# Half a part's weights turned as bf16 halves, and the accumulator scaled by VectorE

## The reference, cut to what matters

```python
h = maximum(layernorm(x), 0)
q, k, v = h @ Wq.T + bq, h @ Wk.T + bk, h @ Wv.T + bv
scores = where(adj > 0, q @ k.T / sqrt(128), -9e15)
x = x + elu(softmax(scores) @ v)            # first layer
h = maximum(layernorm(x), 0)
hw = h @ W                                   # second layer
e = where(adj > 0, leaky_relu(hw @ a1 + (hw @ a2).T), -9e15)
x = x + hw + softmax(e) @ h
```

## Time and profile before

| what | value |
|---|---|
| median of 3 timed runs | 785.39 us (780.93, 785.39, 785.89) |
| the profiled execution | 782.49 us, its span 780.7 us |
| TensorE, matmuls | 728.9 us busy, 93% of the span |
| TensorE, weight loads | 609.6 us, 78% |
| VectorE | 563.2 us, 72% |
| ScalarE | 559.9 us, 72% |
| GpSimd | 417.6 us, 53% |
| DMA | 130.86 MB, 168 GB/s over the span |

### The profile page before, as it was taken

One profiled execution on the slowest core, in us unless ns is written; L12 is line 12 of the kernel. 1 busy time (PEld: TensorE's weight loads), 2 busy tenths in 40 slices (PEclk: granted clock), 3 DMA queues, 4 the chain that ended last, 5 costly groups with the idle time before them and its releaser, 6 DMA issues. The chain is left out here.

```text
span 780.7 us, 18250 instructions
## 1 busy us (share of the span) xinstructions
PE 728.9 (93%) x6229; PEld 609.6 (78%) x6229; DVE 563.2 (72%) x1199; ACT 559.9 (72%) x1095; POOL 417.6 (53%) x317
## 2 busy tenths in 40 slices
PE   4976999999999999999999998585999999999996
PEld 2555888888888888888888887463888888888885
DVE  4857687878787878878787876498585585586572
ACT  5936678687878777777868787584967977977910
POOL 1058599999999999999999973243000000000000
PEclk9988999999999999999999999797999999999999
DMA  6059989999888898989898954650234334423100
GB/s 229 1 162 280 283 212 248 274 232 280 233 280 238 271 253 254 262 247 256 255 259 245 274 112 73 123 103 1 54 69 93 81 73 91 91 64 87 37 10 13
DMA packets 189323, 130.86 MB, mean 168 GB/s; under 512 B 170336, under 2 KB 176992, under 8 KB 181088
## 3 DMA queue, kind: packets, MB, share of 16 engines
q1 hardware_dynamic: 188544, 130.05, 61.4%
q10 hardware_dynamic: 576, 0.26, 0.1%
q0 software_dynamic: 160, 0.00, 0.0%
HBM read 69.47 MB, written 18.87 MB: 113 GB/s over the span
## 5 line engine op out<-in xcount | busy, mean ns | idle before, releaser
L1337 PE MATMUL ps_x<-v,big 128*128 128x258 bf16 x2048 | 232.0, 275 | 2.3 <-issue 2.3
L1337 PEld LDWEIGHTS ps_x<-v,big 128*128 128x128 fp8e4 x2048 | 198.9, 98 | 32.5 <-issue 2.4
L682 DVE CUSTOM_DVE_ANT_0 scores<-ps_s,mask_neg 128x1024 f32<-128x1024 f32 x128 | 155.7, 1217 | 25.5 <-POOL mask_neg L553 17.0
L538 POOL TENSOR_SCALAR mask_bytes<-adj_sb 128x2048 uint8<-128x2048 int32 x64 | 147.5, 2321 | 44.8 <-POOLq L79 40.9
L601 ACT ACTIVATE scores<-scores,neg_max 128x1024 f32<-128x1024 f32 x128 | 146.1, 1143 | 23.3 <-DVE neg_max L688 23.3
L701 DVE TENSOR_TENSOR low<-scores 128x1024 bf16<-128x1024 f32 x96 | 136.0, 1417 | 29.2 <-ACT scores L601 27.0
L553 POOL TENSOR_SCALAR mask_neg<-mask_bytes 128x2048 bf16<-128x2048 uint8 x64 | 150.6, 2354 | 5.4 <-POOL mask_bytes L538 0.4
L812 PE MATMUL ps_acc<-v_parts,hiT 128*128 128x256 bf16 x768 | 141.6, 274 | 5.4 <-DMA lowT<-low 5.1
L615 ACT ACTIVATE hiT<-ps_t 128x512 bf16<-128x512 bf16 (+1 forms) x128 | 103.0, 805 | 56.6 <-PE ps_t L793 54.0
L878 ACT ACTIVATE big<-s_block,s_col 128x512 fp8e4<-128x512 f32 x224 | 139.3, 714 | 0.0
L813 PE MATMUL ps_acc<-v_parts,lowT 128*128 128x128 bf16 x768 | 134.7, 220 | 0.0
(11 more groups left out here) (139 smaller groups left out, 997.3 us busy)
## 6 DMA issues: line engine op xcount, KB each, us to landing
adj_sb<-in_adj SPq DMA_DIRECT2D x64, 1024.0 KB, 5.3
mask_bytes_dram<-mask_bytes SPq DMA_DIRECT2D x32, 512.0 KB, 2.8
x_sb<-in_x SPq DMA_DIRECT2D x8, 256.0 KB, 7.7
out<-res SPq DMA_DIRECT2D x32, 64.0 KB, 1.5
lowT<-low SPq DMA_TRANSPOSE x96, 4.7
big<-mask_bytes_dram SPq DMA_TRANSPOSE x32, 4.5
raw_w<-in_L_gnn_Wq ACTq DMA_DIRECT2D x1, 64.0 KB, 3.1
raw_w<-in_L_gnn_Wk ACTq DMA_DIRECT2D x1, 64.0 KB, 3.6
```

What stands on the lines that cost most here:

```text
L538: nc.gpsimd.tensor_scalar(mask_bytes[b % 2][:, half(h)], adj_sb[h][:], 1.0, 0.0, ALU.min, ALU.max).then_inc(bytes_ready, 1)
L682: nc.vector.tensor_tensor_reduce(out=scores[bn % 2][:, part(k)], in0=ps_s[k % 2][:], in1=mask[bn % 2][:, part(k)], scale=1.0, scalar=LOWES ...
L1337: last = nc.tensor.matmul(ps_x[b % 2][k][:], by_key_tile(m, t)[:, b], v1[k][:, t, :].bitcast(BF16), start=(t == 0), stop=(t == T - 1))
```

## The change

The fourth part's second half (columns 3584 to 4095) is handled like the other parts. TensorE turns its bf16 high half with four bf16 transposes instead of four fp32 ones; VectorE makes its low half with a `low_part` of 512 columns (`low3`) before it is turned, and SP turns that by DMA (`lowT3`, 128 KB), issued ahead of the next strip's `lowT0`. Of the two `turned_low` of a strip one is left. `times_v(s, 1)` now waits for `lowT3`. `low_part(s+1, 0)` moves behind `add_mask(s+2, 1)`; `low_part(s+1, 3)` takes its place.

The accumulator is no longer copied by ScalarE. VectorE's `attended(s-1)` takes each half of it from PSUM with a scalar_tensor_tensor, which scales it by one over the sum and adds bv to the first and the first result to the second. It stands where `turned_low(s, 1)` stood. The next strip's first `times_v` waits for it (`att_ready`). GpSimd's `add_halves` is gone.

ELU's minus one is taken from x in the first stage, by GpSimd, a chunk of 512 columns at a time, once a chunk is normalised; `add_elu` no longer subtracts ones.

```diff
@@ -96,6 +96,10 @@
...
+            for c in range(NC if x_in else 0):
+                pool.wait_ge(h_ready, c + 1)
+                xs = x_sb[:, 4 * c:4 * c + 4, :]
+                nc.gpsimd.tensor_scalar(xs, xs, -1.0, None, ALU.add)
@@ -430,17 +434,18 @@
...
+            UNITS = ((3, slice(0, 512)), (3, slice(512, PART)), (0, slice(0, PART)), (1, slice(0, PART)),
+                     (2, slice(0, 512)), (2, slice(512, PART)))
...
+                hiT = [sb(c2, f"hiT{k}", [D, PART], BF16) for k in range(3)] + [sb(c2, "hiT3", [D, 512], BF16)]
+                low = [sb(c2, f"low{k}", [D, PART], BF16) for k in range(3)] + [sb(c2, "low3", [D, 512], BF16)]
+                lowT = [sb(c2, f"lowT{k}", [D, 8, D], BF16) for k in range(3)] + [sb(c2, "lowT3", [D, 4, D], BF16)]
@@ -493,11 +498,11 @@
                     def turn_low(c, b, k):
...
-                        sp.wait_ge(low_done, 3 * s + k + 1)
+                        sp.wait_ge(low_done, 4 * s + 1 + (1, 2, 3, 0)[k])
...
-                            sp.wait_ge(pv_done, 8 * s + 2 * k - 4)
+                            sp.wait_ge(pv_done, 8 * s + (-4, -2, 0, -6)[k])
@@ -506,6 +511,7 @@
...
+                    turn_low(0, 0, 3)
                     turn_low(0, 0, 0)
...
                         if has(c, b, 1):
+                            turn_low(*at(c, b, 1), 3)
                             turn_low(*at(c, b, 1), 0)
@@ -552,21 +559,10 @@
...
-                    def add_halves(s):
...
-                        nc.gpsimd.tensor_tensor(acc_sb[:, 0, :], acc_sb[:, 0, :], acc_sb[:, 1, :], ALU.add).then_inc(halves_added, 1)
...
-                        nc.gpsimd.tensor_tensor(att[:], acc_sb[:, 0, :], bv_rep[:], ALU.add).then_inc(att_ready, 1)
...
-                        steps = Steps(pool, pool_own, 2 * s)
+                        steps = Steps(pool, pool_own, s)
                         pool.wait_ge(att_exp_ready, s + 1)
-                        steps.do(nc.gpsimd.tensor_tensor(att_exp[:], att_exp[:], ones[:], ALU.subtract))
                         steps.do(nc.gpsimd.tensor_tensor(att_exp[:], att_exp[:], att_pos[:], ALU.add))
                         xs = x_sb[:, s, :] if isinstance(s, int) else x_sb[:, bass.ds(s, 1), :].rearrange("p o f -> p (o f)")
...
                 @block.scalar
...
-                    def copy_pT(s, i):
...
-                        nc.scalar.activation(pT_high[i][:], ps_t[i % 3][:], ACT.Copy).then_inc(pT_ready, 1)
...
-                    def acc_copy(s, b):
...
-                        nc.scalar.activation(acc_sb[:], ps_a[:], ACT.Copy, scale=inv_by_parity[:, b % 2:b % 2 + 1]).then_inc(acc_out, 1)
+                        k, half_of = UNITS[u]
+                        act.wait_ge(t_done, TURNS * s + 1 + u)
+                        wait(act, pv_done, 8 * s + (-7, -6, -4, -2, 0, 0)[u])
+                        if u == 0:
+                            nc.scalar.activation(pT_high[:], ps_t[0][:], ACT.Copy).then_inc(hiT_ready, 1)
+                        else:
+                            out = hiT[3][:] if u == 1 else hiT[k][:, half_of]
+                            nc.scalar.activation(out, ps_t[u % 3][:].bitcast(BF16)[:, half_of], ACT.Copy).then_inc(hiT_ready, 1)
@@ -688,24 +668,33 @@
...
                     def low_part(s, b, k):
                         dve.wait_ge(exp_done, 4 * s + EXP_ORDER.index(k) + 1)
                         wait(dve, lowT_in[k], 16 * s)
-                        p = scores[b % 2][:, part(k)]
+                        p = scores[b % 2][:, part(k) if k < 3 else slice(N - 512, N)]
                         nc.vector.tensor_tensor(low[k][:], p, high_half(p), ALU.subtract).then_inc(low_done, 1)
+                    def turned_low(s):
+
+                        dve.wait_ge(hiT_ready, TURNS * s + 1)
+                        nc.vector.tensor_tensor(pT_low[:], ps_t[0][:], pT_high[:], ALU.subtract).then_inc(pT_low_ready, 1)
+
                     def inverse_sum(s, b):
-                        steps = Steps(dve, own, s)
-                        steps.do(nc.vector.tensor_reduce(out=inv_sum[:, b % 2:b % 2 + 1], in_=row_sum[:, b, :], axis=AX.X, op=ALU.add))
-                        wait(dve, acc_out, s - 1)
-                        nc.vector.reciprocal(inv_by_parity[:, b % 2:b % 2 + 1], inv_sum[:, b % 2:b % 2 + 1]).then_inc(inv_ready, 1)
+                        steps = Steps(dve, own, 2 * s)
+                        steps.do(nc.vector.tensor_reduce(out=inv_sum[:, 0:1], in_=row_sum[:, b, :], axis=AX.X, op=ALU.add))
+                        steps.do(nc.vector.reciprocal(inv_by_parity[:, 0:1], inv_sum[:, 0:1]))
+
+                    def attended(s):
+
+                        dve.wait_ge(pv_done, 8 * s + 8)
+                        nc.vector.scalar_tensor_tensor(out=acc_sb[:], in0=ps_a[:, 1, :], scalar=inv_by_parity[:, 0:1],
+                                                       in1=bv_rep[:], op0=ALU.mult, op1=ALU.add).then_inc(acc_half, 1)
+                        wait(dve, att_exp_ready, s)
+                        dve.wait_ge(acc_half, s + 1)
+                        nc.vector.scalar_tensor_tensor(out=att[:], in0=ps_a[:, 0, :], scalar=inv_by_parity[:, 0:1],
+                                                       in1=acc_sb[:], op0=ALU.mult, op1=ALU.add).then_inc(att_ready, 1)
@@ -728,11 +718,12 @@
                         ahead, ahead2 = has(c, b, 1), has(c, b, 2)
                         if has(c, b, -1):
                             inverse_sum(s - 1, (b + 3) % 4)
-                        turned_low(s, 0)
+                        turned_low(s)
                         low_part(s, b, 1)
                         if ahead:
                             add_mask(s + 1, bn, 2)
-                        turned_low(s, 1)
+                        if has(c, b, -1):
+                            attended(s - 1)
                         low_part(s, b, 2)
                         if ahead:
                             add_mask(s + 1, bn, 3)
@@ -743,12 +734,15 @@
                             dve.wait_ge(epi_done, s - 2)
                             moments_of(s - 3)
                         if ahead:
-                            low_part(s + 1, bn, 0)
+                            low_part(s + 1, bn, 3)
                         if ahead2:
                             add_mask(s + 2, (b + 2) % 4, 1)
+                        if ahead:
+                            low_part(s + 1, bn, 0)
                     all_periods(dve, period)
                     inverse_sum(T - 1, 3)
+                    attended(T - 1)
@@ -768,47 +762,41 @@
...
-                    def turn(s, b, i):
...
-                            col = 512 * (6 + i) + D * t
-                            last = nc.tensor.transpose(ps_t[i % 3][:, D * t:D * t + D], scores[b % 2][:, col:col + D], ident[:])
...
                     def turn_high(s, b, u):
...
-                        k, tiles = ((0, range(8)), (1, range(8)), (2, range(4)), (2, range(4, 8)))[u]
+                        k, half_of = UNITS[u]
                         pe.wait_ge(exp_done, 4 * s + EXP_ORDER.index(k) + 1)
+                        wait(pe, hiT_ready, TURNS * s + u - 2)
                         if u == 0:
-                            wait(pe, hiT_ready, 4 * s)
-                        elif u < 3:
-                            pe.wait_ge(pT_low_ready, 2 * s + u)
-                        else:
-                            pe.wait_ge(hiT_ready, 4 * s + 1)
-                        out = ps_t[(2 + u) % 3][:].bitcast(BF16)
+                            for t in range(4):
+                                col = 512 * 6 + D * t
+                                last = nc.tensor.transpose(ps_t[0][:, D * t:D * t + D], scores[b % 2][:, col:col + D], ident[:])
+                            last.then_inc(t_done, 1)
+                            return
+                        if u == 3:
+                            pe.wait_ge(pT_low_ready, s + 1)
+                        out = ps_t[u % 3][:].bitcast(BF16)
                         high = high_half(scores[b % 2][:, part(k)])
-                        for t in tiles:
-                            last = nc.tensor.transpose(out[:, D * t:D * t + D], high[:, D * t:D * t + D], ident_half[:])
+                        for col in range(half_of.start, half_of.stop, D):
+                            last = nc.tensor.transpose(out[:, col:col + D], high[:, col:col + D], ident_half[:])
                         last.then_inc(t_done, 1)
                     def times_v(s, i):
                         j = PV_ORDER[i]
-                        if i < 2:
-                            pe.wait_ge(pT_low_ready, 2 * s + i + 1)
-                        else:
-                            pe.wait_ge(hiT_ready, 4 * s + (1, 1, 2, 2, 3, 4)[i - 2])
-                            if i % 2 == 0:
-                                pe.wait_ge(lowT_in[j // 2], 16 * s + 16)
+                        pe.wait_ge(hiT_ready, TURNS * s + (1, 2, 3, 3, 4, 4, 5, 6)[i])
                         if i == 0:
```

(43 more changed lines are left out.)

33 lines of the change are left out of this document (5 added, 28 removed).

## The result

The changed kernel takes 811.98 us (median of four runs, 806.04 to 815.85), the one before beside it 784.08: a ratio of 1.035, 95% interval 1.028 to 1.043. It is slower, by more than the forecast's whole range. Its profiled execution took 806.04 us, 23.5 more than that of before.

The account below looks back on a forecast made before the run. The prediction took TensorE, full at 13.32 us a strip, and an equally long ScalarE-VectorE cycle as the bounds. Start +3, strips -4.6, last transposes -0.2 and end -1.3 gave -3.1 us: 781 from 783.9, range 776 to 792.

Parts of the forecast that it names:

- TensorE's 0.21 per strip: Four fp32 transposes become four bf16 ones: minus 0.21 us per strip, leaving 13.11 of pure TensorE work.
- The failed step: VectorE's new `low_part` of 512 columns takes 0.7 us and lies beside an idle wait for TensorE.
- Rival B: GpSimd's add holds part 2's low part as now, or `low_part(3)` meets `mask_bytes`, costing some tenths: 785 to 792, 14%.
- Rival C: The loads don't come earlier, lowT3 lands late, TensorE waits 0.9 us per strip: +20 us, 803; 4%.
- the load goes earlier with it: On SP's queue: GpSimd ends `mask_bytes` 1.4 to 2.4 us earlier, so the adjacency load ahead of lowT3 is issued earlier.
- there after 5 to 6: lowT3 lands 5 to 6 us after the strip's start, in time by half a microsecond.
- The cycle through `attended`: From a strip's first `times_v` round to `attended` and back: 13.18 us, with release 0.06 and `attended` 0.35 + 0.03 + 0.35.
- the whole expected gain of 4.6 us: In the steady strips: 13.16 us each, 0.16 less over 29 strips, 4.6 us in all.
- Part 2's low part: On VectorE: gets the port 0.12 us before the second `mask_neg` starts, and takes 1.22 instead of 1.70.
- Rival A: The second `mask_neg` starts before part 2's low part, which ends 1.88 us later: strips of 14.8, 825 us; 12%.
- Start and end: The first strips cost +3 us behind the wait for lowT3; the end after the last strip gains 1.3.
- The tail that the forecast priced: After the last strip, the copy, two adds and subtraction (2.1 us) give way to 0.73: -1.3 us.

Follow-up runs that it names:

- experiment 5: The changed kernel with the epilogue of before (ScalarE copies and scales the accumulator, five adds on GpSimd), only the turn changed: 800.23 us, 1.0172.
- experiment 7: The kernel of experiment 1 with `attended` put ahead of `add_mask(s+1,2)`: 788.73 us, 1.0051.
- experiment 11: Changed kernel, experiment 1's waits from later strips on, `attended` before `add_mask`, lowT3 between the loads, first transposes ahead of the fourth strip's loads: 778.78 us, 0.9926.
- experiment 1: The changed kernel with GpSimd's first `mask_neg` and second `mask_bytes` made to wait for part 1's and part 3's low parts: 792.27 us, 1.0074.
- experiment 2: The changed kernel without lowT3's DMA transpose, a constant zero in its place: 798.49 us, 1.0167.
- experiment 3: The changed kernel with lowT3 issued between the two adjacency loads and the first strip's transposes ahead of the fourth's loads: 796.51 us, 1.0145.
- experiment 8: The kernel of experiment 7 with `mask_neg` waiting for `turned_low` instead, and neither GpSimd instruction yielding in the first strips: 826.29 us, 1.0525.
- experiment 9: The kernel of experiment 11 without its two waits on GpSimd: 832.44 us, 1.0628.
- the sixth experiment: The changed kernel with each GpSimd instruction of 2048 columns cut into two of 1024: 798.39 us, 1.0173.

## Why the prediction was wrong

- **TensorE's 0.21 per strip** was nearly right: 13.11 forecast, 13.13 in the strips where nothing else binds (experiments 5, 7, 11).
- **The failed step** is `low_part(3)`, "0.7 by L694's 0.69 for 512, and lies beside an idle wait for TensorE". Its duration alone was right (0.67). Its port was not worked out: the rule that the same text applies to part 2's low part holds for every new instruction with two SBUF inputs. It came 0.09 after the second `mask_bytes`, waited 1.7, and what follows it on VectorE (`add_mask`, part 0's low part, the next `turned_low`, and with them `attended`) came late. Rival B named this very meeting and priced it at "some tenths", the size of a missed slot instead of the rest of a 1.9 us instruction. It costs 0.33 per strip against the 13.33 of experiment 1, about 9 us, and by experiment 5 it costs this only together with `attended`.
- **Rival C**, 4%, came true in part. TensorE waited for lowT3 in few strips and briefly, but without these waits the long strips behind them are gone too, 13 to 15 us in all (experiments 2, 3). That "the load goes earlier with it" was right: lowT3 is issued 0.32 before a strip's first turn (350.78 against 351.10), where lowT0 stood 1.96 behind it. The landing was mis-sized: "there after 5 to 6" took lowT0's 5.9, but lowT3, just behind the load, took 6.3 to 9.1 (between the loads, in experiment 3, mostly 2.9), so it landed mostly 6 to 7.4 after the strip's start, and TensorE wanted it at about 7 (344.43 in the strip from 337.45).
- **The cycle through `attended`** was under-sized: 13.18 forecast, 13.34 in the first experiment's rows, with release 0.15 instead of 0.06 and `attended` 0.80 instead of 0.73 to its end (0.10 stands between its two instructions, not 0.03). These 0.16 are the whole expected gain of 4.6 us; so even without collisions the strip stays near before's 13.32.
- **Part 2's low part** was right: 1.22, by a margin of 0.04 where 0.12 was forecast. Rival A, the same race lost, is what experiments 8 and 9 show: strips of 14.72, where 14.8 was worked out, for 0.03 us.
- **Start and end**: +3.4 for the first two strips (forecast +3). The end is +1.2, not -1.3. The tail that the forecast priced came as it said: from TensorE's last product (516.3) to the last add (519.0) 2.7 us, where before had 3.9. But the last strip's first `times_v` now waits for part 1's low part and `attended` on VectorE, and starts 6.97 behind the strip's first turn, before 5.12. TensorE had been idle for 3.66 us, and the granted clock fell to 0.50 behind it, its level of 1.2 GHz, where before kept 1.00 from 483 to 487: a matmul takes 0.37 to 0.42 instead of 0.27. The forecast had neither term. The matmul, and the row of 507 to 511 us in the form of rows 1:

```profile
507.63 0.37 PE L800 MATMUL ps_acc<-v_parts,pT_high 128*128 128x256 bf16 x1 [3.66 <-DVE att L696]
...
507.00:511.00 4.00, 3.37 (x24) 2.87 (x25) 1.94 (x6) 1.02 (x1) 0.00 (x0) 0.50 0.64 123
```

What stays open: how a wait of 0.26 for lowT3 becomes a strip of 15.3 three strips on was read from the rows, not shown by a run that moves one phase alone. Nor is it shown why the first strip of the loop's body is some 0.36 late (13.67 against 13.33 in experiment 1), or why `mask_neg` starts first in three early strips even without any lowT3. The parts don't add up exactly either: 9 + 13 + 3.6 for start and end is 26 against 23.5, each from another run.

## What to carry to other kernels

Where two engines share a port and whoever starts first keeps it, price every new instruction that needs it by whose instruction runs at its start, and the loser by the whole rest of that instruction; a margin of 0.1 us in a race for it is no margin. A held instruction lengthens the kernel only where the next thing on the critical path waits behind it: two held low parts were free while ScalarE scaled the accumulator, and not once VectorE did. A wait that orders the two engines can be worth more than it costs, if it stands behind the right event, and the mean time of the held instructions says nothing until it is known whether that engine is on the path. When a DMA is added to an in-order queue, look at what the issue ahead of it waits for, not only at the bytes.

## What was not expected of the hardware

The race is decided within hundredths of a microsecond: 0.04 ahead of GpSimd's second `mask_neg` costs nothing, 0.03 behind it 1.72 us. The Trainium skill (SBUF — State Buffer, Who interferes with whom) calls the shared port an exclusive lock; these rows agree, and so does the sixth experiment, where halving GpSimd's instruction cuts the longest wait (2.80 to 2.08). Back to back, a queued GpSimd instruction leaves nearly no gap for VectorE: two `mask_bytes` take 3.75 together, 1.89 each. Two VectorE instructions of which the second waits for the first by a semaphore start 0.45 apart at 0.35 each, where two without such a wait overlap by 0.08 (342.38 and 342.83, then 343.10).
